# A conditioned GRU over 512 steps: the update gate's recurrent product in two f16 halves, moved behind two groups of projections

## What is computed

```
vz, vr, vh = video @ C_z + b_z, video @ C_r + b_r, video @ C + b
xz, xr, xh = seq @ W_z, seq @ W_r, seq @ W            # for every step
def step(h, (xzt, xrt, xht)):
    z = sigmoid(xzt + h @ U_z + vz)
    r = sigmoid(xrt + h @ U_r + vr)
    hh = tanh(xht + (r * h) @ U + vh)
    h_new = (1 - z) * h + z * hh
out = x + all h_new
```

## Time and profile before

| | |
|---|---|
| median of 3 runs | 2472.28 us (2469.28 to 2473.05) |
| the profiled execution's own time | 2469.78 us |
| its span, first to last instruction | 2468.0 us |
| busy: PE, DVE, ACT, POOL | 97%, 63%, 32%, 26% |
| mean granted TensorE clock | 0.991 of full |

### The profile page before, as it was taken

One profiled execution on the slowest core, in us unless ns is written; L12 is line 12 of the kernel. 1 busy time (PEld: TensorE's weight loads), 2 busy tenths in 40 slices (PEclk: granted clock), 3 DMA queues, 4 the chain that ended last, 5 costly groups with the idle time before them and its releaser, 6 DMA issues.

```text
span 2468.0 us, 166186 instructions
## 1 busy us (share of the span) xinstructions
PE 2390.1 (97%) x74366; PEld 2074.1 (84%) x74366; DVE 1544.1 (63%) x6617; ACT 787.9 (32%) x2571; POOL 632.5 (26%) x1165
## 2 busy tenths in 40 slices
PE   2999999999999999999999999999999999999998
PEld 1888888888888888888888888888888888888887
DVE  3666656666566665666656666566665666666665
ACT  2333333333333333333333333333333333333322
POOL 0222222222222222222222222222222222222222
PEclk8999999999999999999999999999999999999999
DMA  9010110110101101101101111011011011011000
GB/s 192 22 39 22 39 39 22 39 34 26 40 22 38 39 21 40 38 21 39 38 23 38 31 29 38 23 38 39 22 38 40 21 39 38 22 38 38 21 21 21
DMA packets 145969, 87.90 MB, mean 36 GB/s; under 512 B 9024, under 2 KB 140608, under 8 KB 145216
## 3 DMA queue, kind: packets, MB, share of 16 engines
q1 hardware_dynamic: 145216, 76.84, 12.2%
HBM read 43.25 MB, written 33.55 MB: 31 GB/s over the span
## 4 chain that ended last, share of the span: by engine, by line
PE 96%; issue 1%; SPq 1%; DVE 1%; DMA 1%; ACT 0%; POOLq 0%; POOL 0%; DVEq 0%
PE banks L208 55%; PE p_bank L216 40%; DMA w_stage<-in_L_cond_W_z_dram 1%; SPq L120 0%; SPq L115 0%; SPq L126 0%; DVE h_t L473 0%; DVE w_top L394 0%; DVE taken L467 0%; PE p_bank L224 0%; ACT gate_c L324 0%; DVE state L471 0%; DVE w_lo L407 0%; ACT w_hi L311 0%; SPq L123 0%
## 5 line engine op out<-in xcount | busy, mean ns | idle before, releaser
L216 PE MATMUL p_bank<-w_hi,x_t 128*32 128x384 f16 x16384 | 1122.1, 327 | 7.1 <-issue 7.0
L208 PE MATMUL banks<-u,h_t 128*32 128x128 f32 x32768 | 1004.1, 274 | 18.7 <-issue 16.8
L208 PEld LDWEIGHTS banks<-u,h_t 128*32 128x32 f32 x32768 | 912.9, 110 | 73.5 <-issue 23.9
L216 PE MATMUL p_bank<-w_lo,x_t 128*32 128x384 f16 x8192 | 739.2, 327 | 0.5 <-issue 0.5
L216 PEld LDWEIGHTS p_bank<-w_hi,x_t 128*32 128x32 f16 x16384 | 510.2, 97 | 115.3 <-issue 9.9
L208 PE MATMUL banks<-u,reset_t 128*32 128x128 f32 x16384 | 554.4, 274 | 2.8 <-issue 2.3
L455 DVE TENSOR_TENSOR reset<-gate_r,state 128x64 f32<-128x64 f32 x1024 | 226.7, 221 | 509.6 <-ACT gate_r L319 509.6
L208 PEld LDWEIGHTS banks<-u,reset_t 128*32 128x32 f32 x16384 | 442.2, 109 | 87.1 <-DVE reset_t L457 35.8
L187 POOL TENSOR_TENSOR result<-x_nat,state 128x128 f32<-128x128 f32 x512 | 235.4, 460 | 939.6 <-DVE state L471 939.6
L181 POOL TENSOR_TENSOR kept<-keep,state 128x128 f32<-128x128 f32 x512 | 236.0, 461 | 875.3 <-ACT keep L321 875.3
L388 DVE SCALAR_TENSOR_TENSOR banks<-p_bank,x_down,base 128x128 f32<-128x128 f32 x1536 | 429.4, 341 | 6.3 <-PE p_bank L216 4.2
(11 more groups left out here) (39 smaller groups left out, 419.9 us busy)
## 6 DMA issues: line engine op xcount, KB each, us to landing
x_nat<-in_x_dram SPq DMA_DIRECT2D x256, 128.0 KB, 2.9
out_dram<-result SPq DMA_DIRECT2D x256, 128.0 KB, 2.7
c_w<-in_L_cond_C_r_dram SPq DMA_DIRECT2D x4, 256.0 KB, 6.4
c_w<-in_L_cond_C_z_dram SPq DMA_DIRECT2D x4, 256.0 KB, 9.1
c_w<-in_L_cond_C_dram SPq DMA_DIRECT2D x4, 256.0 KB, 11.8
w_stage<-in_L_cond_W_r_dram SPq DMA_DIRECT2D x4, 256.0 KB, 14.6
w_stage<-in_L_cond_W_z_dram SPq DMA_DIRECT2D x4, 256.0 KB, 16.6
w_stage<-in_L_cond_W_dram SPq DMA_DIRECT2D x4, 256.0 KB, 17.1
```

The lines of the kernel that those rows point to most:

```text
L208: last = nc.tensor.matmul(out[part(j)], turned[:, part(q)], weights[:, q, cols(j)], start=first and q == 0, stop=q == Q - 1, skip_group_ch ...
L216: last = nc.tensor.matmul(p_bank[k][part(j), 0:G * N], x_t[set_][:, c, part(q), a], w[b][:, :, q, cols(j)], start=f == 0, stop=f == GROUPS ...
```

## The change

The update product is no longer f32. `U_z` is scaled and split at the start like a W (it becomes the first of four matrices in `SPLITS`, and its load moves ahead of the W's). In each step ACT writes `h_hi`, the f16 high half of 2^14 x h_t, and DVE `h_lo`, the rest; `update_product` adds h_hi x uz_hi, h_hi x uz_lo and h_lo x uz_hi: 48 f16 matmuls of 128 columns where the f32 product has 32 records. The seeds of the update gate are scaled up to match, and the two sigmoids scale down (`z_down`, `z_minus`).

On PE the two projection groups now come between the reset product and the update product. On DVE the seed of the next step's R comes first in the step, then h_lo; the seeds of Z and C stay behind the transposes of reset. The work on x is spread: sums in steps 7 and 0, total in 1, scale in 2, 3 and 4 in small pieces, scaled x on ACT in 3 and 5, its high half in 4 and 6, POOL's low half behind 4 and 6, and a transpose of one step's x in every step, between kept and taken on DVE. `x_t_ready` is waited for in every step.

```diff
-    SUM_STEPS, TOTAL_STEP, SCALE_STEP, SPLIT_STEPS, TURN_STEPS = (0, 1), 2, 3, (3, 5), (5, 7)
+    SUM_STEPS, TOTAL_STEP, POWER_STEP, UP_STEP, DOWN_STEP = (7, 0), 1, 2, 3, 4
+    WHOLE_STEPS, HIGH_STEPS, TURN_AHEAD = (3, 5), (4, 6), 3
+    UZ = G
+    SPLITS = (UZ, R, Z, C)
...
+        uz = [sb(n, [P, Q, E], f16) for n in ("uz_hi", "uz_lo")]
+        h_hi, h_lo = sb("h_hi", [P, N], f16), sb("h_lo", [P, N], f16)
+        z_up, z_down, z_minus = sb("z_up", [P, 1]), sb("z_down", [P, 1]), sb("z_minus", [P, 1])
...
+            load_weights(u[:, Z], U_z, s_u_in[Z])
             for g, m in enumerate((W_r, W_z, W_h)):
                 load_weights(w_stage[:, g], m, s_w_in[g])
-            for g, m in enumerate((U_r, U_z, U_h)):
-                load_weights(u[:, g], m, s_u_in[g])
+            load_weights(u[:, R], U_r, s_u_in[R])
+            load_weights(u[:, C], U_h, s_u_in[C])
...
-                if t in SPLIT_STEPS and not (last and j == BODY - 1):
-                    k = SPLIT_STEPS.index(t)
+                if t in HIGH_STEPS and not (last and j == BODY - 1):
+                    k = HIGH_STEPS.index(t)
                     rest_of_x(k, 2 * n + 3 + k if first or last else pool.snap(2 * n + (3 + k)))
...
+            def update_product(out, now):
+                pe.wait_ge(h_hi_ready, now)
+                for a, b in PARTS:
+                    if a == 1:
+                        pe.wait_ge(h_lo_ready, now)
+                    for q in range(Q):
+                        for j in range(J):
+                            last = nc.tensor.matmul(out[part(j)], (h_hi, h_lo)[a][:, part(q)], uz[b][:, q, cols(j)],
+                                                    start=False, stop=q == Q - 1, skip_group_check=True)
+                return last
...
-                product(cell(k, Z), h_t, u[:, Z]).then_inc(z_mm, 1)
                 m, c = divmod(tt + 2, SET)
                 j, t = divmod(tt, BLOCK)
                 if fill:
                     if t == TOTAL_STEP and not (last and j == BODY - 1):
                         blocks = i * BODY + j + 2
                         total_x(j + 1, blocks)
-                    if c == 0:
-                        sets = i * (STEPS // SET) + m + 1
-                        pe.wait_ge(x_t_ready, sets if last else pe.snap(sets))
+                    pe.wait_ge(x_t_ready, s + 3 if last else pe.snap(s + 3))
                     project(k, c, 0, BEFORE_C, m % 2)
+                update_product(cell(k, Z), now).then_inc(z_mm, 1)
                 product(cell(k, C), reset_t, u[:, C], halves=[(reset_t_ready, a) for a in halves]).then_inc(c_mm, 1)
...
-            def split_x(n, k, turned, before):
-                tile = x_nat[n % BUFS][:, k * SET:(k + 1) * SET]
+            def whole_x(n, k, before):
+                if before is not None:
+                    act.wait_ge(x_lo_ready, before)
+                nc.scalar.activation(x_whole[:], x_nat[n % BUFS][:, k * SET:(k + 1) * SET], ACT.Copy,
+                                     scale=x_up[n % 2][:]).then_inc(x_whole_ready, 1)
+
+            def high_x(n, k, turned):
                 if turned is not None:
                     act.wait_ge(x_t_ready, turned)
-                if before is not None:
-                    act.wait_ge(x_lo_ready, before)
-                nc.scalar.activation(x_whole[:], tile, ACT.Copy, scale=x_up[n % 2][:])
-                nc.scalar.activation(x_parts[k][:, :, 0], tile, ACT.Copy, scale=x_up[n % 2][:]).then_inc(x_hi_ready, 1)
+                nc.scalar.activation(x_parts[k][:, :, 0], x_nat[n % BUFS][:, k * SET:(k + 1) * SET], ACT.Copy,
+                                     scale=x_up[n % 2][:]).then_inc(x_hi_ready, 1)
...
+                act.wait_ge(h_t_ready, HALVES * (s + 1) if last else act.snap(HALVES * s + HALVES))
+                nc.scalar.activation(h_hi[:], h_t[:], ACT.Copy, scale=2.0 ** POW).then_inc(h_hi_ready, 1)
                 act.wait_ge(r_mm, now)
                 nc.scalar.activation(gate_r[:], cell(k, R), ACT.Sigmoid).then_inc(r_gate, 1)
                 act.wait_ge(z_mm, now)
-                nc.scalar.activation(keep[:], cell(k, Z), ACT.Sigmoid, scale=-1.0).then_inc(z_keep, 1)
-                nc.scalar.activation(gate_z[:], cell(k, Z), ACT.Sigmoid).then_inc(z_gate, 1)
+                nc.scalar.activation(keep[:], cell(k, Z), ACT.Sigmoid, scale=z_minus[:]).then_inc(z_keep, 1)
+                nc.scalar.activation(gate_z[:], cell(k, Z), ACT.Sigmoid, scale=z_down[:]).then_inc(z_gate, 1)
...
+                if t == SUM_STEPS[0] and more(2):
+                    b, u_ = divmod(j + 2, BUFS)
+                    act.wait_ge(x_in[u_], count(16 * J * (i * (BODY // BUFS) + b + 1)))
+                    sum_x(j + 2, 0, count(2 * n + 4))
+                if t == SUM_STEPS[1] and more(1):
+                    sum_x(j + 1, 1, count(2 * n + 3))
+                if t in WHOLE_STEPS and more(1):
+                    k = WHOLE_STEPS.index(t)
+                    if k == 0:
+                        act.wait_ge(x_scaled, count(n + 2))
+                    whole_x(j + 1, k, count(2 * n + (2 + k)))
+                if t in HIGH_STEPS and more(1):
+                    k = HIGH_STEPS.index(t)
+                    high_x(j + 1, k, count(BLOCK * n + (SET + SET * k)))
...
-            def turn_x(k, sets):
+                V.tensor_scalar(x_down[k][:], w_down[:, 0:G], x_pow[k][:], None, ALU.mult).then_inc(x_link, 1)
+
+            def turn_x(k, c, sets):
                 dve.wait_ge(x_lo_ready, sets)
-                V.transpose(x_t[k][:].rearrange("p c n a -> p (c n a)").bitcast(i32),
-                            x_parts[k][:].rearrange("p n a -> p (n a)").bitcast(i32)).then_inc(x_t_ready, 1)
-
-            def seed(k, d):
-                for g in range(G):
+                V.transpose(x_t[k][:, c].rearrange("p n a -> p (n a)").bitcast(i32),
+                            x_parts[k][:, cols(c)].rearrange("p n a -> p (n a)").bitcast(i32)).then_inc(x_t_ready, 1)
+
+            def seed(k, d, gates):
+                for g in gates:
                     last = V.scalar_tensor_tensor(cell(k, g), p_bank[k][:, cols(g)], x_down[d][:, g:g + 1], base[:, g],
                                                   ALU.mult, ALU.add)
-                last.then_inc(seeded, 1)
-
-            def top_of_w(g):
-                dve.wait_ge(s_w_in[g], 16 * J)
-                V.tensor_reduce(w_top[:, g:g + 1], w_stage[:, g], AX.XY, ALU.max, apply_absolute_value=True)\
+                    if g == C:
+                        last.then_inc(seeded, 1)
...
+            def scales_of_z():
+                link(V.tensor_copy(z_down[:], w_down[:, UZ:UZ + 1]))
+                link(V.tensor_scalar(z_minus[:], z_down[:], -1.0, None, ALU.mult))
+                link(up_of(z_up[:], w_pow[:, UZ:UZ + 1], 2 * POW))
+                link(V.tensor_scalar(base[:, Z], base[:, Z], z_up[:], None, ALU.mult))
+                dve.sem_inc(s_z_scale, 1)
...
+            for m in range(1, G + 1):
+                top_of_w(m)
+                rest_of_w(m - 1)
+            rest_of_w(G)
+            link(V.tensor_scalar(w_down[:, Z:Z + 1], w_down[:, Z:Z + 1], z_up[:], None, ALU.mult))
...
-                if more and t == SCALE_STEP:
+                ahead = (tt + 1) % 2, (tt + 1) // BLOCK % 2
+                if not (last and tt == STEPS - 1):
+                    if t == BLOCK - 1:
+                        dve.wait_ge(x_link, count(4 * n + 8))
                     dve.wait_ge(projected, count(s + 2))
-                    scale_x((j + 1) % 2, n + 1, count)
+                    seed(*ahead, (R,))
+                dve.wait_ge(h_hi_ready, now)
+                V.scalar_tensor_tensor(h_lo[:], h_t[:], 2.0 ** POW, h_hi[:], ALU.mult, ALU.subtract)\
+                    .then_inc(h_lo_ready, 1)
+                if more and t == POWER_STEP:
+                    power_x((j + 1) % 2, n + 1, count)
+                if more and t == UP_STEP:
+                    up_x((j + 1) % 2, n + 1, count)
+                if more and t == DOWN_STEP:
                     scale_down((j + 1) % 2)
-                if more and t in TURN_STEPS:
-                    k = TURN_STEPS.index(t)
-                    turn_x(k, count(2 * n + (3 + k)))
 
                 dve.wait_ge(r_gate, now)
                 for a in range(HALVES):
@@ -457,12 +516,12 @@
                     V.transpose(reset_t[:, half(a)], reset[:, half(a)]).then_inc(reset_t_ready, 1)
 
                 if not (last and tt == STEPS - 1):
-                    if t == BLOCK - 1:
-                        dve.wait_ge(x_link, count(4 * n + 8))
-                    dve.wait_ge(projected, count(s + 2))
-                    seed((tt + 1) % 2, (tt + 1) // BLOCK % 2)
-
+                    seed(*ahead, (Z, C))
                 dve.wait_ge(kept_ready, now)
+                if not (last and tt >= STEPS - TURN_AHEAD):
+                    m, c = divmod(tt + TURN_AHEAD, SET)
+                    turn_x(m % 2, c, count(i * (STEPS // SET) + (m + 1)))
```

(47 more changed lines are left out.)

51 lines of the change are left out of this document (29 added, 22 removed).

## The result

The changed kernel takes 2621.84 us, the median of four runs (2605.06 to 2626.81), against 2472.26 (2469.28 to 2473.05): a ratio of 1.0595, interval 1.0547 to 1.0644. It is slower, as forecast, but by 150 us and not by 13. The profiled execution took 2626.81, its span is 2625.0, 157 us above that of before.

What follows compares the result with a forecast made beforehand. PE was taken as the bound (96% of the path that ended last), with two chains almost as long. Terms: 2469.8 + 4 steady + 5.9 start-up + 3 code = 2482.7; the median lies 2.5 higher: 2485 us, range 2450 to 2512.

Steps and rivals of the forecast that it cites:

- Update product: On PE: 48 f16 matmuls, priced by columns, take 0.66 us where the f32 product took 0.875.
- order on PE: Reset, two projection quads, update, then candidate product, which waits for reset_t; ordinary step 4.51 us.
- h_hi: ACT's extra copy after h_t's second half: 0.30 us, done before gate_r is due.
- the early seed: On DVE, R's seed moves ahead of h_lo: no cost in six steps of eight.
- C0: Start of the candidate product on PE, forecast 1.99 us after the step's first reset matmul in six steps of eight.
- h_lo behind POOL: In two steps of eight POOL holds h_lo on DVE: reset 0.38 us late, step 4.89.
- keep, gate_z, kept, and the x transposes: Work behind the later update product and in DVE's gap: ends before it is needed, costs nothing.
- Sum of the steady part: Block of eight steps: 36.84 us against 36.78, +4 us over 64 blocks.
- Start-up: U_z takes a fourth turn on DVE before the first projection: +5.9 us, bounds 4.7 to 7.
- Code: PE's code queue: 320 records a step, not 288, so more packets and less time for each: +3 us (0 to 10).
- code arrives too late: Rival, 20%: PE's code packets need about 3.0 us; a 0.2 stall in four steps costs 26 us, giving 2508.
- Half of the gain given to the reset chain: On PE: half of what the shorter update product saves is lost waiting for reset_t before the candidate product.

Runs made afterwards that it cites:

- e5: Changed kernel with POOL making x's low half in pieces of 128 columns, one behind each step's reset: 2574.41 us.
- e11: Kernel before the change with 16 more tiny PE records a step (304): 2501.35 us.
- e3: Kernel before the change with 32 more tiny PE records a step (320), into unused PSUM columns: 2568.78 us.
- e9: Changed kernel without the loads and stores of x in the middle of the run: 2510.89 us.
- e6: Changed kernel with h_hi meeting uz_hi and uz_lo in one matmul of 256 columns, halves added on DVE, 288 records a step: 2521.95 us.
- e1: Changed kernel without the third part of the update product (h_lo x uz_hi), 288 records a step: 2533.44 us.
- e2: Changed kernel with the update product in f32 again, at its new place and behind the same waits, 288 records a step: 2590.82 us.
- e7: Changed kernel with merged h_hi matmuls, POOL's low half in pieces, and x's loads and stores in pairs two steps apart: 2457.87 us.
- e10: e7 written out in passes of 256 steps, so that no engine jumps back: 2513.86 us.
- e12: Kernel before the change written out in passes of 256 steps, so that no engine jumps back: 2499.55 us.

## Why the prediction was wrong in size

*Update product, order on PE, h_hi, the early seed.* Right: 0.66, C0 at 1.99, h_hi 0.31 for 0.30, an ordinary step of 4.513 to 4.517 for 4.51.

*h_lo behind POOL.* Right in kind, and a little too dear. Reset began at R0+1.73 and not +1.81: DVE's record of reset starts 0.08 before that of h_lo ends, so the two overlap, which the spacing of the seeds hadn't shown. The step is 4.80, median 4.79, for 4.89. e5 shows the cost by taking it away.

*keep, gate_z, kept, and the x transposes.* Right: nothing of them is on the chain.

*Sum of the steady part.* 6 x 4.515 + 2 x 4.79 = 36.67 a block for 36.84; with the steps of the table -8 us for +4. So the change would be 8 us faster in its steady part, if code came in time.

*Start-up.* 7.3 for 5.9, just above its upper bound of 7: the first load landed 2.1 later, 41.12 for 38.99, and only part of this was made up.

*Code.* This step failed: +3, with 10 as its upper bound, where lateness took 144 and the pass changes 13. The working counted the packets rightly and took scattered lateness as something that grows with their number. What decides is the time per packet against the 3.6 us that a packet needs from one bound to the next (1.17 until it starts, 1.06 to land, 1.40 until PE goes on): at 4.01 a packet there is some room for one that starts late, at 3.60 there is none. e11 and e3 show the bend: 9 us for the first 16 records and 36 for the next. The second rival, *code arrives too late*, had the mechanism, and its chance of 20% was too low; its price of 26 was too low by a factor of about six. It put a packet's need at 3.0 us, where it is 3.6, held that against the fastest 256 instructions of a step, and let one stall of 0.2 come in four steps. In the trace a stall like that of 1200.44 takes 1.43: a packet that meets x's transfers comes over 1 us late (5.11 for 3.65 behind the one before it), and PE has no second packet in reserve from which to make it up. That the DMA engines are shared stood in the rival in half a sentence, without a price; e9 gives it: 103 of the 161.

*Half of the gain given to the reset chain* was right as well, and is why a faster product could bring so little: all that the split could save on PE was 0.015 us a step with the held steps, 0.08 without them (e5).

That records per time are the main cause, and not the split, the order or the waits, is shown by e6: the same product in the same place, 32 records fewer, one more operation and wait on DVE, and lateness 20 for 161. That traffic of x is a condition of most of it is shown by e9. Not settled: why e1 and e2, with 288 records and packets of 3.98 and 4.12, have a lateness of 70 and 56, most of it in steps 0 and 1, when e6 and e7 have 20 at 4.06 and 3.97. At e1's and e2's stalls the packets had started late as well, 2.05 and 2.00 behind the bound (medians) for 1.06 and 0.96 at their other bounds, so the stalls are of the same kind, but why so many packets are late there is open. Where the packets' bounds fall against the moves of x could do it; no run varied that alone. What happens in the 1.1 to 1.6 us between a landing and PE's next record isn't shown either.

## What to carry to other kernels

A split into half-precision parts trades columns for instructions. Before pricing it by columns, divide the time of a step by its records and compare with the code queue: here PE ran with 17 us of lateness at 4.0 us per 256 records, with 26 at 3.83, and with 137 to 161 at 3.6 with transfers beside it. Even 4.0 is not safe: e1, e2, e10 and e12 had 56 to 86 at 3.98 to 4.12. If the parts share a stationary operand, merge them into one wider matmul and add later on an engine with room, which here was worth 100 us. And don't leave an operation with two SBUF inputs in a chain on DVE beside a long one of POOL: cutting POOL's into pieces took 0.28 off each held step here (e5).

## What the runs showed that I had not expected

- Late code isn't one stall a packet but, in the stretch shown, mostly one every 4 or 5 packets, of 0.5 to 1.7 us between starts, always at a multiple of 256 records, with the clock granted in full throughout (1.00 in the windows above).
- The jumps back at a pass's end cost 28 us for seven in the kernel before and 41 after. But written out without jumps both kernels are slower, by 31 us (before) and 56 (e7).
- 48 matmuls of 128 columns with their loads start within 0.66, 14 ns apart, in the four strips.
- DVE's reset started 0.08 before the recorded end of the h_lo ahead of it, and h_lo itself ended 0.15 behind POOL (1227.67 and 1227.52), though it needs 0.29 when nothing holds it.
